# A vision tower's attention: one of 64 score blocks per image exponentiated by GpSimd and VectorE, and three steps taken off TensorE

## What is computed

```python
h = patches(x) @ W.T + b + pos                      # 16 x 1024 x 64
n = layernorm(h)
scores = q @ k.T / sqrt(8) + col_bias               # per head 1024 x 1024
h = h + softmax(scores) @ v @ Wo + bo
n = layernorm(h)
combine = top2(softmax(n @ router_w.T))             # 1024 x 8
h = h + n + sum_e combine[:, e] * (gelu(n @ w1[e] + b1[e]) @ w2[e] + b2[e])
```

## Time and profile before

| | |
|---|---|
| time, median of 3 runs | 1130.87 us (1130.76 to 1132.0) |
| the profiled execution's own time | 1132.75 us |
| its span, first to last instruction | 1130.7 us |
| attention phase (exponentials) | about 48 to 991 us |
| expert phase | about 991 to 1131 us |
| busy: PE, ACT, DVE, POOL | 96%, 91%, 55%, 12% of the span |

### The profile page before, as it was taken

How to read it: one execution, slowest core, us unless ns; L and a number is a source line. 1 busy time by engine, 2 the same in 40 slices (tenths; PEclk the granted TensorE clock), 3 DMA queues, 4 the chain that set the end, 5 groups by cost and what they waited for, 6 DMA issues and landing times.

```text
span 1130.7 us, 21748 instructions
## 1 busy us (share of the span) xinstructions
PE 1086.5 (96%) x7803; PEld 318.6 (28%) x7804; DVE 623.4 (55%) x1765; ACT 1026.2 (91%) x1127; POOL 130.8 (12%) x137
## 2 busy tenths in 40 slices
PE   3499999999999999999999999999999999999998
PEld 3122222222222222222222222222222222233333
DVE  8423465646464737374646465554646542476865
ACT  1299999999999999999999999999999999976654
POOL 3304011111111110102010101010101101000000
PEclk9899999999999999999999999999999999999999
DMA  2523131314141414241423232232323136049895
GB/s 55 128 59 67 55 85 46 88 41 109 30 119 31 107 43 105 46 105 46 104 46 95 56 94 56 74 76 66 84 58 76 42 85 152 16 136 241 236 246 164
DMA packets 73794, 100.78 MB, mean 89 GB/s; under 512 B 17276, under 2 KB 30076, under 8 KB 73660
## 3 DMA queue, kind: packets, MB, share of 16 engines
q1 hardware_dynamic: 71404, 98.73, 34.6%
q10 hardware_dynamic: 1776, 0.24, 0.1%
q0 software_dynamic: 480, 0.06, 0.1%
HBM read 57.67 MB, written 40.37 MB: 87 GB/s over the span
## 4 chain that ended last, share of the span: by engine, by line
PE 77%; ACT 10%; issue 6%; DVE 3%; DMA 2%; SPq 0%; ACTq 0%; POOL 0%; DVEq 0%; POOLq 0%
PE psum L1653 37%; PE psum L1637 21%; ACT probs L1369 10%; PE psum L1706 4%; PE psum L1730 4%; PE psum L743 2%; DMA m_cT<-cT_d 2%; PE psum L731 1%; PE psum L747 1%; PE psum L767 1%; PE psum L772 1%; PE psum L737 1%; PE psum L753 1%; PE psum L1716 1%; DMA x_d<-x2T 0%
## 5 line engine op out<-in xcount | busy, mean ns | idle before, releaser
L1369 ACT ACTIVATE probs<-psum 128x1024 f32<-128x1024 f32 x1024 | 941.1, 1241 | 26.5 <-PE psum L1637 26.4
L1653 PE MATMUL psum<-probs,VA 128*32 128x512 f32 x4096 | 547.0, 606 | 1.9 <-ACT probs L1369 0.4
L1637 PE MATMUL psum<-QA,KA 54*128 54x512 bf16 x2048 | 331.6, 385 | 8.4 <-issue 3.6
L1637 PEld LDWEIGHTS psum<-QA,KA 54*128 54x128 bf16 x2048 | 82.0, 93 | 484.9 <-ACT probs L1369 447.1
L1441 DVE STREAM_TRANSPOSE oT<-psum 128x512 f32<-128x512 f32 x64 | 45.9, 717 | 202.3 <-PE psum L1653 201.8
L1653 PEld LDWEIGHTS psum<-probs,VA 128*32 128x32 f32 x4096 | 81.8, 108 | 151.9 <-issue 130.9
L1404 ACT ACTIVATE probs<-psum,b 128x1024 f32<-128x1024 f32 x64 | 68.1, 1111 | 41.0 <-PE psum L1706 40.9
L1706 PE MATMUL psum<-m_x,w 64*128 64x512 f32 x256 | 61.6, 596 | 2.9 <-DMA m_cT<-cT_d 2.7
L1548 DVE TENSOR_TENSOR probs<-probs,psum 128x1024 f32<-128x1024 f32 x32 | 39.1, 1220 | 33.8 <-PE psum L1716 31.1
L1730 PE MATMUL psum<-probs,w 128*64 128x512 f32 x240 | 57.3, 598 | 0.0
L1308 POOL TENSOR_TENSOR p_rstd<-p_ve,neg_half 128x8 f32<-128x8 f32 x16 | 32.9, 2055 | 207.2 <-DVE p_ve L468 207.2
(11 more groups left out here) (180 smaller groups left out, 813.6 us busy)
## 6 DMA issues: line engine op xcount, KB each, us to landing
H_all<-comb_d SPq DMA_DIRECT2D x64, 256.0 KB, 5.5
QA<-q_parts_d SPq DMA_DIRECT2D x64, 192.0 KB
KA<-k_parts_d SPq DMA_DIRECT2D x64, 192.0 KB
q_parts_d<-qk_parts SPq DMA_DIRECT2D x32, 192.0 KB, 2.5
k_parts_d<-qk_parts SPq DMA_DIRECT2D x32, 192.0 KB, 2.7
xT<-in_xT SPq DMA_DIRECT2D x16, 256.0 KB, 2.7
q_parts_d<-qk_parts SPq DMA_DIRECT2D x32, 128.0 KB, 2.6
k_parts_d<-qk_parts SPq DMA_DIRECT2D x32, 128.0 KB, 2.5
```

The source lines that it names most:

```text
L1369: nc.scalar.activation(probs[:, k % PROB_BUFS, :], score_buf(buf_of(k)), ACT.Exp).then_inc(exped, 1)
L1637: last = pe.matmul(score_buf(buf_of(k))[:, (g % 2) * BANK:(g % 2 + 1) * BANK], KA[rows_of(h, SCORE_ROWS), h // 2, jt * P:(jt + 1) * P], QA ...
L1653: last = pe.matmul(o_acc[32 * g:32 * g + 32, :], VA[:, jt, h, :], probs[:, k % PROB_BUFS, (g % 2) * BANK:(g % 2 + 1) * BANK], start=(jt == ...
```

## The change

- Of each image, the second block of quad 15 is no longer exponentiated by ScalarE. TensorE computes its two heads' scores in the extra bank in slots 0 and 1 (`side_0`, `side_1`); VectorE reads them out times log2(e); GpSimd rounds (`side_round`), VectorE takes the fraction (`side_fraction`, slot 3), GpSimd evaluates a polynomial with four steps of tensor_scalar and tensor_tensor (`side_terms`) and builds the power of two (`side_power`), and VectorE multiplies the two (`side_product`, slot 15). TensorE's values of quad 15 in slot 17 wait for that.
- `post_t` and, from the third image on, `norm_t` leave TensorE: VectorE turns 32x32 blocks in place (`turn_x2`, `turn_normal`) and a store and a load through DRAM move the blocks. The opening still has its two `norm_t`.
- The router runs in one slot instead of two, with tokens in the columns, and VectorE turns its result.
- The slots of nearly all steps move; among them the squares now come ahead of the subtraction, tokens are centred at slot 8 rather than 6, and are added and turned at slot 11 rather than 26.
- The combine weights are stored with one transfer instead of four, in another order, so that the broadcast loads of the expert phase read runs of 128 numbers instead of 512.

```diff
+SIDE_QUADS = (15,)
+EXPS = [(q, half) for q in range(QUADS) for half in range(2) if not (half and q in SIDE_QUADS)]
+AUX_SLOTS = {0: ("side_0", 0), 1: ("side_1", 0), 2: ("qk0", 0), 4: ("qk0", 1), 5: ("out_proj", 0), 7: ("out_proj",
+             1), 10: ("qk1", 0), 12: ("qk1", 1), 16: ("sq", 0), 18: ("router", 0), 21: ("embed", 0), 23:
+             ("embed", 1), 26: ("v", 0), 28: ("v", 1), 30: ("combine_t", 0)}
+FRACTION_SLOTS, POWER_SLOTS = (3,), (15,)
-CENTRE_SLOT, SCALE_SLOT, SPLIT_SLOT, SHIFT_SLOT, LEAD_SLOT, NORM_SLOT = 6, 10, 13, 20, 23, 28
+CENTRE_SLOT, SCALE_SLOT, SPLIT_SLOT, SHIFT_SLOT, LEAD_SLOT, NORM_SLOT = 8, 10, 14, 20, 24, 25
-G_SLOT = 26
+G_SLOT = 11
...
+            def load_normal(n):
+                sp.wait_ge(xn_stored, 16 * QUARTERS * (n - 1))
...
+                sp.dma_start(xnT[:, n % 2, :], xn_d[n]).then_inc(xn_loaded, 16)
...
-                for c in range(NCH // 2):
-                    sp.dma_start(comb_d[bq].rearrange("t (r c i) -> c r t i", c=NCH // 2, i=32)[c],
-                                 combB[32 * c:32 * c + 32, :, :]).then_inc(comb_stored, 16)
+                sp.dma_start(comb_d[bq].rearrange("t (p i) -> p t i", i=32), combB[:, :, :]).then_inc(comb_stored, 16)
...
+            def side_round(b, side):
...
+                g.tensor_scalar(side_n[:, :], side_y[:, n % 2, :], ROUNDER, None, ALU.add).then_inc(side_rounded, 1)
+            def side_terms(b, side, first, last):
...
+                for c in range(first, last - 1, -1):
+                    if c == 4:
+                        g.wait_ge(side_split, n + 1)
+                        g.tensor_scalar(side_p[:, :], side_f[:, :], POWER_TERMS[5], POWER_TERMS[4], ALU.mult,
+                                        ALU.add).then_inc(side_chain, 1)
+                    else:
+                        g.tensor_scalar(side_p[:, :], side_p[:, :], POWER_TERMS[c], None, ALU.add).then_inc(side_chain, 1)
+                    g.wait_ge(side_chain, base + 2 * (4 - c) + 1)
+                    g.tensor_tensor(side_p[:, :], side_p[:, :], side_f[:, :], ALU.mult).then_inc(side_chain, 1)
+                    g.wait_ge(side_chain, base + 2 * (4 - c) + 2)
+            def side_power(b, side):
...
+            def side_fraction(b, side):
+                n = SIDES * b + side
+                v.wait_ge(side_rounded, n + 1)
+                v.scalar_tensor_tensor(side_f[:, :], side_n[:, :], ROUNDER, side_y[:, n % 2, :], ALU.subtract,
+                                       ALU.subtract).then_inc(side_split, 1)
+            def side_product(b, side):
+                n = SIDES * b + side
+                v.wait_ge(side_ready, n + 1)
+                v.scalar_tensor_tensor(side_n[:, :], side_p[:, :], POWER_TERMS[0], side_y[:, n % 2, :], ALU.add,
+                                       ALU.mult).then_inc(side_done, 1)
...
                 for e in range(2):
-                        sp.dma_start(wgt_rows[i][D * e:D * e + D, :].rearrange("p (t n) -> p t n", t=2),
-                                     comb_d[b].rearrange("t (e n) -> e t n", e=NX)[2 * m + e].partition_broadcast(D)).then_inc(rows_spread[i], 16)
+                        sp.dma_start(wgt_rows[i][D * e:D * e + D, :].rearrange("p (g n) -> p g n", n=P),
+                                     comb_d[b].rearrange("t (a e n) -> e (t a) n", a=QUARTERS, e=NX)[2 * m + e].partition_broadcast(D)).then_inc(rows_spread[i], 16)
...
                 def body(b):
+                    side_round(b, 0)
+                    if b:
+                        g.wait_ge(pv_done, QUADS * b)
+                        alone(g)
+                        copy_v(1)
                     add_bo(b)
+                    side_terms(b, 0, 4, 3)
                     if b:
                         post_pow(b - 1)
+                    side_terms(b, 0, 2, 1)
+                    side_power(b, 0)
...
+                    if q in SIDE_QUADS:
+                        pe.wait_ge(side_done, SIDES * b + SIDE_QUADS.index(q) + 1)
```

More of the change, by code:

```diff
@@ L101, in step_of @@
     step, part = AUX_SLOTS[slot]
[L102 removed]
+    image = b + (2 if step in LEAD else 1 if step in PREP else 0 if step in SIDE else -1)
     return (step, part, image) if 0 <= image < NB else None
@@ L740, in aux_step @@
                     rows = slice(D * int(step[-1]), D * int(step[-1]) + D)
+                    if step == "qk0" and n >= 2:
+                        pe.wait_ge(xn_loaded, 16 * (n - 1))
                     for i in halves:
                         cols = slice(i * BANK // 2, (i + 1) * BANK // 2)
-                        last = pe.matmul(aux[:, cols], w_qk[rows, :, :].rearrange("k a e -> k (a e)"), xnT[rows, cols],
+                        last = pe.matmul(aux[:, cols], w_qk[rows, :, :].rearrange("k a e -> k (a e)"), xnT[rows, n % 2, cols],
                                          start=True, stop=True)
```

331 lines of the change are left out of this document (212 added, 119 removed).

## The result

The changed kernel took 1248.66 us (median of 4, 1247.87 to 1253.63) against 1131.43 us (1130.76 to 1132.48) for the kernel before: a ratio of 1.104, with a 95% interval of 1.102 to 1.106. It is slower, as forecast, but by 117 us and not by 21, far outside the range of 1113 to 1178.

What follows compares the result with a forecast made beforehand. ScalarE was taken to bound attention, TensorE the expert phase. Fourteen images at 2.6 lost less 0.92 gained, less 2 x 0.92 and 0.8, gave +20.9 us on a median of 1130.87: 1152 us, range 1113 to 1178.

Steps and rivals of the forecast that it cites:

- I take 1.17 us for a tensor_scalar of 1024 (bounds 0.9 and 2.0): GpSimd's side work: price of each one-input instruction, from a copy's slope of 1.0 ns for each element.
- The chain behind the root: GpSimd's five side instructions after the tokens' inverse root: 3 x 1.17 + 2 x 2.42 = 8.4 us.
- The root before it: GpSimd's inverse root of the tokens, ahead of the side instructions: forecast to end about 18.8 us into the image.
- the theory of who is late: Attention: VectorE, held up by GpSimd, delivers the product late, at 34.4 us against 31.5 wanted.
- Bound and gain: Attention: ScalarE is the bound; one block fewer takes an image to 57.9 us, 16 x 0.92 = 14.7 us gained.
- Deadlines: Attention: squares wanted at 29.4 us, forecast at 30.0; product wanted at 31.5, forecast at 34.4.
- Exclusion: VectorE's two-input and GpSimd's reading instructions exclude each other; 2.6 us lost for each image (0.4 to 5).
- the forecast of 1152: Whole kernel: likeliest time, 1152 us, with late product and late squares; own range 1134 to 1185, chance 0.55.
- Tensor_tensor at 2.42: GpSimd's side work: a two-input instruction of 1024 takes 2.42 us.
- falls if: Condition for dropping the prediction: GpSimd's tensor_tensor of 1024 takes well under 2.4 us.
- Transfers at nothing: Attention's token loads through DRAM: cost nothing, 0.9 us to spare; 1.5 later costs up to 0.6 for each image.
- Packets: Rival, expert phase: 512-byte packets make it transfer-bound, 6 us more at half again per byte, 36 at twice; chance 0.05.

Runs made afterwards that it cites:

- e13_split19: e8_all with VectorE's residual add and the rest of the q and k split moved to slot 19, behind the router's logits; 1116.9 us.
- e5_fast: The changed kernel with GpSimd's round, three polynomial additions and power all written as mult-then-add; 1188.0 us.
- e12_one_input: e8_all with GpSimd's four two-tensor multiplications in the polynomial replaced by cheap one-input instructions (wrong exponentials); 1123.7 us.
- e4b_no_chain: The changed kernel with GpSimd's polynomial and power cut to three instructions (wrong exponentials); 1134.8 us at the median.
- e8_all: e5_fast with expert weights stored in 4 KB rows, the last x2 load issued later and normalised tokens loaded right behind their store; 1172.6 us.

## Why the prediction was wrong

**The step that failed** is "I take 1.17 us for a tensor_scalar of 1024 (bounds 0.9 and 2.0)". I read the slope from a copy and took it for all one-input instructions. In the changed kernel the additions took 2.90 us on the mean and the power 4.41; by themselves 2.77 and 3.64. The chain behind the root was 16.2 us and not 8.4: two additions and a power 10.6 in place of 3.5, two multiplications 5.2 against 4.8 expected, the gaps the rest. The root before it ended 20.2 us into the image (from 572.53), where 18.8 was forecast; that is another 1.4. What failed is the size of a term, but it lay outside its bounds, and with it the theory of who is late turned round: the product waited for GpSimd's power, not for VectorE's turn. Only with the cheap forms did VectorE become late, as forecast.

**Bound and gain**: right. With nothing in the way (e13_split19) 63 exponentials take 58.0 us (927.9 / 16), where 57.9 was forecast, and the block is worth 14.9 us of time, where the forecast had 14.7.

**Deadlines**: right as deadlines. But the squares', which was forecast to be missed by 0.6 us, was kept in this kernel (done at 27.7, wanted 29.4); that lateness appeared in e5_fast (13.4 us, 14 times).

**Exclusion**: right in kind, and shown by e12_one_input, casts included: L684 took 1.61 where 0.69 is its time alone, L691 3.26 where 1.22 is. In the kernel after it cost less than GpSimd's forms: its instructions behind the root were longer than alone by 0.24, 0.44, 0.32 and 0.85 us, 1.9 in all. The additions, which the forecast had held up by a tensor_scalar, ran freely (0.72 for two). In e5_fast the loss is (984.8 - 930.2) / 15 = 3.6 us for each image against e4b_no_chain, where the forecast had 2.6, and nearly all of it is exclusion: without the two-input instructions e12_one_input's attention is 51.6 us shorter than e8_all's. So with GpSimd's prices near those that I assumed (e5_fast) the forecast of 1152 would still have met 1188. By an estimate from the runs 15 of the 36 us are this term, 11 the packets, 5 the transfers of attention; 5 are not accounted for. The Trainium skill, SBUF — State Buffer (Who interferes with whom), has whoever issues first hold the shared pair for the whole instruction where VectorE is in a two-port mode, and lets VectorE's two-input instructions contend with GpSimd's reads. The traces agree for GpSimd's two-input instructions (the cast above stood until 558.24). With the dear forms VectorE's two-input instructions stood only at the start (L1582, L727).

**Tensor_tensor at 2.42**: right, 2.37 alone. The prediction's "falls if" was put on the price that held, not on the one that didn't.

**Transfers at nothing**: wrong by 4.7 us, 0.3 for each image, inside the 0.6 that I had allowed. With three more stores ahead of it, this load cost far more.

**Packets**, a rival at 0.05 that should have been a term: 10 to 11 us with 6 forecast for half as much again per byte. The Trainium skill, DMA: Bandwidth & Descriptors (Specifications), has 512 bytes as the smallest transfer at line rate. This case's traces differ: at the same 232 GB/s the engines were busy 0.95 of the time with these packets and 0.86 with longer ones.

**The sum closes like this.** An image of the kernel after took 66.0 us, 8.0 more than the 58.0 of e13_split19; 15 times that, less the 14 us that the block gives, are the 106 us of attention. The wait for the product explains 6.1 of the 8.0. Part of the remainder goes with the granted clock, which was 0.934 of full speed on the mean of the span (0.995 before). Four stretches of the image above, up to the stall, in it, behind it and further on (us, busy PE, PEld, DVE, ACT, POOL, clock, DMA share, GB/s):

```profile
590.00:603.00 13.00, 13.00 (x102) 3.16 (x100) 12.49 (x17) 13.00 (x16) 12.48 (x6) 1.00 0.15 42
603.00:610.30 7.30, 0.57 (x8) 0.16 (x5) 3.77 (x3) 2.87 (x4) 5.82 (x2) 0.86 0.49 138
610.30:622.00 11.70, 11.69 (x80) 2.62 (x80) 7.22 (x24) 8.19 (x10) 0.57 (x1) 0.79 0.49 121
622.00:638.50 16.50, 16.42 (x128) 4.70 (x124) 10.27 (x42) 16.50 (x19) 2.43 (x2) 1.00 0.12 27
```

The clock was at its upper level (1.00, 2.4 GHz) before the stall, while TensorE was busy throughout. On the mean it was 0.86 in the stall, where TensorE was busy 0.57 of 7.3 us, and 0.79 in the 11.7 us behind it, so partly at the lower level of 1.2 GHz, and then at the upper one again. Not all of the low mean is of this kind: the opening (the first 48.4 us) had a clock of 0.68 here and 0.99 before and took as long in both. In e13_split19, without the stalls, the mean is 0.991. What the clock costs by itself no run here separates.

## What to carry to other kernels

Price an instruction by its exact form: an add of a constant, a mult-then-add and a subtract-then-mult of the same tile differed by a factor of 3.5 on GpSimd, and a neighbouring row of another form does not bound it. Where work moves to GpSimd, both its cheap one-input instructions and those with two inputs took time from VectorE here, so put VectorE's work that nobody waits for behind what somebody does, and ask after each mended wait which one is next. Count packets as well as bytes where the DMA engines are as busy as in this expert phase (0.82 before the change).

## What the runs showed of the hardware

- GpSimd's tensor_scalar on 128x1024 f32: mult-then-add 1.04 us, a single add or mult 2.77, subtract-then-mult or add-then-max 3.64. An int32 result costs nothing more. On 128x512 it is 0.62 and 1.50.
- GpSimd's two-input and cheap one-input instructions held up VectorE's: with the two-input ones an addition of 128x256 took 1.48 us on the mean instead of 0.42, and a cast of 128x1024 2.24 instead of 0.69; beside a cheap one two additions took 1.68 instead of 0.72. A dear one-input form held one up only at its start (0.57 us of 3.64).
- Packets of 512 bytes took the DMA engines from 0.86 to 0.95 busy at the same 232 GB/s, and a phase of 140 us became 10 us longer.
- The granted TensorE clock fell from 1.00 to 0.86 in a stall of 7 us and stood at 0.79 in the 11.7 us behind it.
